# Second layer of a graph stack: attention weights a step later, updates two, half of the moments taken one layer earlier

## The chip, the cores and the metric

One core of a Trainium2 chip runs the whole kernel. The metric is device time in microseconds. TensorE does matrix products, VectorE (DVE), ScalarE (ACT) and GpSimd (POOL) the rest; each takes its own instructions in order and waits on semaphores for the others.

## The reference

64 graphs of 128 nodes with 256 features pass through four layers; each adds to x what it makes of h = relu(layernorm(x)). The second layer is the one at issue:

```python
h  = einsum(h, W); s1 = h @ a1; s2 = h @ a2
e  = leaky_relu(s1[:, :, None] + s2[:, None, :], 0.2) * mask
att = softmax(e, axis=2)
x  = x + elu(att @ h + beta * h)
```

The first layer is (adjT * q k^T) / row norm @ v, the third a normalised adjacency times h times a weight plus a bias, the fourth masked attention with 8 heads. All are float32 to the outside.

## The kernel before, in words

All of x lies in SBUF (`xs`). The graphs are worked in 32 pairs, p = 0 to 31, one layer after the other. There is no scheduler: the order on each engine is the order in which the step functions write their calls, and semaphores that count pairs tie the engines together. Several pairs are in flight, since an engine's step p handles p on one item and p - 1, p - 3 on others.

**Layer norm ahead.** For each pair VectorE takes `moments` (L114, two bn_stats), `mean_variance` (L120) and `root_argument` (L127, two small operations on mean and variance); GpSimd takes the inverse root by a power of -0.5 (`inverse_root` L140) and centres and scales (`centre` L223, two instructions of 128x256) into one of two buffers `xnb`; TensorE transposes, ScalarE takes the relu.

**First layer** (from L276). VectorE's step (L628): low part of the relu (L578), low part of the turned relation (L590), moments three pairs ahead, mask (L583), update of x (L600), low part of the values (`low_v` L595). TensorE's (L375) is t_product, turn, turn_relation, values (which needs `low_v` of the pair before), relation, outputs. VectorE's steps from p = 7 run in a hardware loop (L647), as do TensorE's and ScalarE's. GpSimd's step (L508) has the root, the norm's root, the centring. The last three steps of VectorE (L650 on) take the second layer's moments of pairs 0, 1 and 2.

**Second layer** (from L668), all written out. Per step p:
- TensorE (L714): `product(p)`, transposes of the attention weights of p - 2 (`turn_prob`), transposes of pair p + 1 (`turn`), `spread(p)` (transposes that lay out s2; it waits for ScalarE's copy of the product and for VectorE's masked scores of p - 1), `attend(p - 2)`.
- ScalarE (L772): copy of the product (`copy_h` L742, which writes `val`), copy of the turned weights, relu of the next pair, `elu_negative(p - 3)`, `softmax_exp(p - 1)`, `elu_exp(p - 3)`.
- VectorE (L859): `mask_max(p - 1)` (masked scores L832, leaky L837 whose two inputs are both `masked_e`, maximum L840), moments, aggregate and arguments of pair p + 3, reciprocal (L844), attention weights (L850, two instructions, inputs `exp_e` and `beta_ident`), update `elu(p - 4)` (L856, one input in PSUM).
- GpSimd (L812): root of pair p + 2, centring of it, `add(p - 4)` (L810: x plus exponential, 128x512, both in SBUF).

`leaky_e`, `exp_e` and `att` are single buffers. The central lines are:

```python
if p >= 1:
    mask_max(p - 1)
dve.wait_ge(freed, when)
moments(dve, ahead, step_sem, (p + 1) % 2)
mean_variance(dve, ahead, step_sem, (p + 1) % 2)
root_argument(dve, ahead, step_sem, ready_sem, (p + 1) % 2)
if p >= 1:
    inverse(p - 1)
    attention(p - 1)
if p >= 4:
    elu(p - 4)
```

## Time and profile before

| what | value |
|---|---|
| runs | 752.18 us median of 3 (751.97 to 753.36) |
| the profiled execution | 750.46 us |
| its span | 748.7 us |
| busy, share of the span | TensorE 94%, VectorE 84%, ScalarE 76%, GpSimd 63% |
| first layer | to about 179 us |
| second layer | about 179 to 323 us |

A profile is one execution. Its rows give when an instruction (or a run of like ones, xN) started and how long it took; neighbours on one engine can overlap a little, so the distance from start to start is what an instruction costs its engine. In brackets stands how long the engine had been idle before, and who released it.

### The profile page before, as it was taken

Reading aid. Unit: us, or ns where it says so; the run is one execution under the profiler, and the core shown is the slowest. Engines: PE = TensorE matmul, PEld = TensorE weight load, DVE = VectorE, ACT = ScalarE, POOL = GpSimd, SP = SyncE. Lnnn points to the kernel's source line nnn. Section 1 sums busy time; section 2 is a strip of 40 time slices with the busy share of each in tenths; the row PEclk is TensorE's granted clock in tenths of the full one; section 3 lists DMA queues with packets and bytes.
Section 4 is the critical chain, followed back from the end, with each engine's and each line's share of the span. In section 5 each row is a group of like instructions: output and inputs, shape, how many; then the busy total and the mean of one; then the engine's idle time right before and its main releaser. Section 6 shows DMA issues by size and latency. Waiting matters only on the chain.

```text
span 748.7 us, 22968 instructions
## 1 busy us (share of the span) xinstructions
PE 705.6 (94%) x6938; PEld 653.9 (87%) x6938; DVE 626.1 (84%) x2648; ACT 566.9 (76%) x1900; POOL 473.3 (63%) x610
## 2 busy tenths in 40 slices
PE   6999999998999999779998999999999999999995
PEld 5999999997777777679998899999999999999984
DVE  5888778776899999879998888888888888888863
ACT  3665655654777787747664999999999999999985
POOL 2445445445578778478884766667666676667652
PEclk9999999999999999989999999999999999999999
DMA  7222300000000000000000000000000000000001
GB/s 235 94 84 92 98 0 0 0 0 1 1 1 2 1 2 1 0 1 0 0 0 1 17 16 29 28 28 22 20 28 28 28 15 28 28 28 28 14 29 44
DMA packets 21683, 20.16 MB, mean 27 GB/s; under 512 B 2432, under 2 KB 21632, under 8 KB 21632
## 3 DMA queue, kind: packets, MB, share of 16 engines
q1 hardware_dynamic: 19440, 18.16, 7.6%
q10 hardware_dynamic: 2192, 1.44, 0.7%
q8 instruction: 17, 0.28, 0.2%
q14 instruction: 34, 0.28, 0.1%
HBM read 11.21 MB, written 8.39 MB: 26 GB/s over the span
## 4 chain that ended last, share of the span: by engine, by line
PE 76%; DVE 16%; issue 3%; ACT 2%; POOL 1%; DMA 1%; DVEq 0%; POOLq 0%; ACTq 0%
PE bank L255 42%; PE bank L1076 8%; PE bank L1068 5%; PE bank L1086 4%; PE bank L325 4%; PE bank L154 4%; PE bank L235 3%; PE bank L335 3%; DVE stats L117 3%; DVE xs L856 2%; DVE masked_e L832 2%; DVE leaky_e L837 2%; DVE att L850 2%; DVE small L840 2%; PE bank L245 1%
## 5 line engine op out<-in xcount | busy, mean ns | idle before, releaser
L1146 ACT ACTIVATE prob<-wide,small 128x128 f32<-128x128 f32 x512 | 199.1, 395 | 19.8 <-DVE small L1233 19.8
L1198 POOL TENSOR_TENSOR prob<-prob,small 128x512 f32<-128x512 f32 x128 | 133.3, 1042 | 108.1 <-DVE small L1247 108.1
L143 POOL TENSOR_TENSOR rstd<-vare,mhalf 128x2 f32<-128x2 f32 x128 | 88.8, 694 | 60.0 <-DVE vare L132 60.0
L1233 DVE CUSTOM_DVE_ANT_0 wide<-bank,mbias 128x128 f32<-128x128 f32 x512 | 116.1, 283 | 10.0 <-PE bank L1068 10.0
L226 POOL TENSOR_SCALAR xn<-xs,nmean,rstd 128x256 f32<-128x256 f32 x184 | 101.3, 561 | 11.2 <-POOL rstd L143 10.6
L117 DVE BATCH_NORM_STATS2 stats<-xs 128x6 f32<-128x256 f32 (+1 forms) x256 | 95.5, 415 | 5.7 <-DMA xs<-in_x_dram 4.5
L1146 ACT ACTIVATION_READ_ACCUMULATOR prob<-wide,small 128x1 f32 x512 | 98.3, 192 | 0.0
L1153 ACT COPY probT<-bank 128x512 f32<-128x512 f32 x128 | 72.0, 588 | 6.2 <-PE bank L1076 1.3
L1076 PE MATMUL bank<-ident,prob 128*128 128x128 f32 x512 | 73.9, 276 | 2.3 <-POOL prob L1198 2.3
L492 POOL TENSOR_TENSOR rnorm<-norm,mhalf 128x2 f32<-128x2 f32 x32 | 22.1, 690 | 79.3 <-ACT relsq L433 79.3
L1076 PEld LDWEIGHTS bank<-ident,prob 128*128 128x128 f32 x512 | 57.0, 140 | 9.6 <-issue 5.9
L245 PE MATMUL bank<-w,hT 128*128 128x258 f32 x256 | 61.3, 381 | 1.2 <-DVE xs L604 1.0
L255 PE MATMUL bank<-w,yTs 128*128 128x256 f32 x384 | 55.9, 297 | 4.5 <-DVE xs L980 4.5
L154 PE MATMUL bank<-ident,xn 128*128 128x128 f32 x376 | 56.8, 274 | 0.0
L245 PEld LDWEIGHTS bank<-w,hT 128*128 128x128 f32 x256 | 48.3, 190 | 8.9 <-DVE xs L604 1.2
L255 PE MATMUL bank<-wo,oTs 128*128 128x256 f32 x384 | 53.8, 289 | 2.2 <-DVE oTs L1256 2.2
L255 PEld LDWEIGHTS bank<-w,yTs 128*128 128x128 f32 x384 | 50.1, 199 | 6.0 <-DVE yTs L975 4.8
L255 PE MATMUL bank<-hTs,wq 128*128 128x256 f32 x384 | 53.2, 287 | 0.2 <-DVE hTs L1251 0.2
L255 PE MATMUL bank<-wv,hTs 128*128 128x256 f32 x384 | 52.9, 286 | 0.0
L255 PEld LDWEIGHTS bank<-wo,oTs 128*128 128x128 f32 x384 | 47.2, 188 | 6.3 <-DVE oTs L1256 2.7
L255 PE MATMUL bank<-hTs,wk 128*128 128x256 f32 x384 | 50.7, 281 | 0.0
L422 ACT CAST oTs<-bank 128x512 fp32r<-128x512 f32 x32 | 18.8, 589 | 40.6 <-PE bank L335 40.6
(141 smaller groups left out, 1823.6 us busy)
## 6 DMA issues: line engine op xcount, KB each, us to landing
out_dram<-xs SPq DMA_DIRECT2D x32, 256.0 KB, 2.1
xs<-in_x_dram SPq DMA_DIRECT2D x29, 256.0 KB, 2.7
xs<-in_x_dram ACTq DMA_DIRECT2D x1, 512.0 KB, 7.4
xs<-in_x_dram ACTq DMA_DIRECT2D x1, 256.0 KB, 3.7
wq<-in_L_gnn_Wq_dram SPq DMA_DIRECT2D x1, 256.0 KB, 3.3
wk<-in_L_gnn_Wk_dram ACTq DMA_DIRECT2D x1, 256.0 KB, 4.6
wv<-in_L_gnn_Wv_dram SPq DMA_DIRECT2D x1, 256.0 KB, 5.9
w<-in_L_gnn_W_dram SPq DMA_DIRECT2D x1, 256.0 KB, 7.2
```

Of the source, the lines that this page charges most:

```text
L117: ins = nc.vector.bn_stats(stats[:, b, g, :], x_of(p, g))
L143: nc.gpsimd.tensor_tensor(rstd[:, b, :], vare[:, b, :], mhalf[:, :], ALU.pow).then_inc(rstd_ready, 1)
L154: ins = nc.tensor.transpose(pe_ps[:, c * 2 * N + g * N:c * 2 * N + (g + 1) * N], src[:, g, c * 128:(c + 1) * 128], ident[:, :])
L226: ins = nc.gpsimd.tensor_scalar(xnb[b][:, g, :], x_of(p, g), nmean[:, b, g:g + 1], rstd[:, b, g:g + 1], ALU.add, ALU.mult)
L245: ins = nc.tensor.matmul(ps_g, hT[:, c, g, :], weight[:, c, :], start=(c == 0), stop=(c == C - 1))
L255: ins = nc.tensor.matmul(ps, lhsT(a, c), rhs(b, c), start=(n == 0), stop=(n == len(terms) - 1))
L1068: ins = nc.tensor.matmul(SS[r][:, (g * C + c) * N:(g * C + c + 1) * N], qT[rows_r, c, g, :], kT[rows_r, c, g, :], start=True, stop=True)
L1076: ins = nc.tensor.transpose(PT[r % 2][:, i * N:(i + 1) * N], prob[:, r, i, :], ident[:, :])
L1146: ins = nc.scalar.activation(prob[:, r, i, :], wide[:, r, i, :], ACT.Exp, bias=nmax[r][:, i:i + 1], scale=-1.0, accum_out=rsum[r][:, i:i + 1])
L1153: nc.scalar.copy(probT[:, r, :, :].rearrange("p i n -> p (i n)"), PT[r % 2][:, :]).then_inc(pt_ready, 1)
L1198: nc.gpsimd.tensor_tensor(prob[:, r, :, :], prob[:, r, :, :], rinv[r].unsqueeze(2).to_broadcast([128, QUAD, N]), ALU.mult).then_inc(prob_r ...
L1233: nc.vector.tensor_tensor_reduce(out=wide[:, r, i, :], in0=SS[r][:, i * N:(i + 1) * N], in1=mbias[:, :], scale=-1.0, scalar=3e38, op0=ALU. ...
```

## The change

The second layer's steps reach further back: TensorE turns and attends p - 3 instead of p - 2, ScalarE's ELU parts are those of p - 4, VectorE's update is that of p - 6, GpSimd's add that of p - 5. `leaky_e`, `exp_e`, `att`, the maxima and the sums get two buffers each. VectorE's step becomes: update, masked scores of p - 1, reciprocal of p - 2, leaky of p - 1, attention weights of p - 2, maximum of p - 1, and then moments: of the odd pairs alone, one graph per step, with aggregate and arguments in even steps. The moments of the even pairs are taken by VectorE in the first layer, behind each odd step (x of that pair is final by then), and GpSimd takes their roots four pairs at a time, in the first layer too. GpSimd's step in the second layer is: root (odd p only), add, centring. VectorE's hardware loop in the first layer is written out.

```diff
+        mhalf = sb("mhalf", [128, 8])
+        stats_even = sb("stats_even", [128, 2, 6])
+        mv_even = sb("mv_even", [128, PAIRS // 2, 2, 2])
+        vare_even = sb("vare_even", [128, PAIRS])
+        nmean_even = sb("nmean_even", [128, PAIRS])
+        rstd_even = sb("rstd_even", [128, PAIRS])
...
-        leaky_e = sb("leaky_e", [128, 2, N])
+        leaky_b = [sb(f"leaky_e{b}", [128, 2, N]) for b in range(2)]
...
-        exp_e = sb("exp_e", [128, 2, N])
-        att = sb("att", [128, 2, N])
+        exp_b = [sb(f"exp_e{b}", [128, 2, N]) for b in range(2)]
+        att_b = [sb(f"att{b}", [128, 2, N]) for b in range(2)]
...
+        def root_even(pool, q):
+
+            pool.wait_ge(l1_even_stats, q + 1)
+            part = slice(8 * q, 8 * q + 8)
+            nc.gpsimd.tensor_tensor(rstd_even[:, part], vare_even[:, part], mhalf[:, :], ALU.pow).then_inc(l1_even_root, 1)
+
+        def root_odd(pool, p):
+
+            inverse_root(pool, p // 2, l1_stats_ready, l1_rstd_ready, (p // 2) % 2)
+
+        def centre_first(pool, p, turned, freed):
+
+            if p % 2:
+                b = (p // 2) % 2
+                pool.wait_ge(l1_rstd_ready, p // 2 + 1)
+                scalars = [(nmean[:, b, g:g + 1], rstd[:, b, g:g + 1]) for g in range(2)]
+            else:
+                pool.wait_ge(l1_even_root, p // 8 + 1)
+                scalars = [(nmean_even[:, p + g:p + g + 1], rstd_even[:, p + g:p + g + 1]) for g in range(2)]
+            pool.wait_ge(turned, freed)
+            for g in range(2):
+                ins = nc.gpsimd.tensor_scalar(xnb[p % 2][:, g, :], x_of(p, g), *scalars[g], ALU.add, ALU.mult)
+            ins.then_inc(l1_xn_ready, 1)
+
+        def moments_even(dve, k):
+
+            dve.wait_ge(l0_x_done, 2 * k + 1)
+            if k > 0:
+                dve.wait_ge(l1_even_step, 2 * k)
+            for g in range(2):
+                ins = nc.vector.bn_stats(stats_even[:, g, :], x_of(2 * k, g))
+            ins.then_inc(l1_even_step, 1)
+            dve.wait_ge(l1_even_step, 2 * k + 1)
+            for g in range(2):
+                ins = nc.vector.bn_aggr(mv_even[:, k, g, :], stats_even[:, g, :])
+            ins.then_inc(l1_even_step, 1)
+            if k % 4 == 3:
+                q, pairs = k // 4, slice(k - 3, k + 1)
+                dve.wait_ge(l1_even_step, 2 * k + 2)
+                mean, var = (mv_even[:, pairs, :, i].rearrange("p k g -> p (k g)") for i in range(2))
+                part = slice(8 * q, 8 * q + 8)
+                nc.vector.scalar_tensor_tensor(nmean_even[:, part], mean, -2.0, mean, ALU.mult, ALU.add)
+                nc.vector.scalar_tensor_tensor(vare_even[:, part], var, EPS, var, ALU.add, ALU.max).then_inc(l1_even_stats, 1)
+
+        def moments_odd(dve, i, g):
+
+            b = i % 2
+            if g == 0 and i < 2:
+                dve.wait_ge(l0_xn_ready, PAIRS - 1 + i)
+            elif g == 0:
+                dve.wait_ge(l1_xn_ready, 2 * i - 2)
+            ins = nc.vector.bn_stats(stats[:, b, g, :], x_of(2 * i + 1, g))
+            if g == 1:
+                ins.then_inc(l1_step, 1)
+                dve.wait_ge(l1_step, 2 * i + 1)
+                for g in range(2):
+                    ins = nc.vector.bn_aggr(mv[:, b, g, :], stats[:, b, g, :])
+                ins.then_inc(l1_step, 1)
+                root_argument(dve, i, l1_step, l1_stats_ready, b)
 
         def gather_nodes(pe, ps, p, src, xn_ready):
...
                 for p in range(1, PAIRS - 2):
                     step(p, p % 2)
+                    if p % 8 == 1 and p > 1:
+                        root_even(pool, p // 8 - 1)
                 for n in range(2):
-                    inverse_root(pool, n, l1_stats_ready, l1_rstd_ready, n)
                     inverse_norm(PAIRS - 3 + n)
-                    pool.wait_ge(tr_done, PAIRS - 1 + n)
-                    centre(pool, n, n, l1_rstd_ready, l1_xn_ready)
+                    if n % 2:
+                        root_odd(pool, n)
+                    centre_first(pool, n, tr_done, PAIRS - 1 + n)
                 inverse_norm(PAIRS - 1)
+                root_even(pool, PAIRS // 8 - 1)
...
-                with dve.Fori(3, PAIRS // 2 - 2) as j:
-                    step(2 * j + 1, 1)
-                    step(2 * j + 2, 0)
+                    if p % 2:
+                        moments_even(dve, p // 2)
+                for p in range(7, PAIRS - 3):
+                    step(p, p % 2)
+                    if p % 2:
+                        moments_even(dve, p // 2)
...
                     low_v(p)
-                    if n < 2:
-                        dve.wait_ge(xn_ready, p + 2)
-                        layer_norm_stats(dve, n, l1_step, l1_stats_ready, n)
+                    if n != 1:
+                        moments_even(dve, p // 2)
+                    else:
+                        moments_odd(dve, 0, 0)
+                        moments_odd(dve, 0, 1)
                 relation_low(PAIRS - 1)
-                dve.wait_ge(l1_xn_ready, 1)
-                layer_norm_stats(dve, 2, l1_step, l1_stats_ready)
+                moments_odd(dve, 1, 0)
                 update(PAIRS - 1)
...
                 def step(p):
                     product(p)
-                    if p >= 2:
-                        turn_prob(p - 2)
+                    if p >= 3:
+                        turn_prob(p - 3)
                     if p + 1 < PAIRS:
                         turn(p + 1)
                     else:
                         gather_nodes(pe, HT, 0, xn, l2_xn_ready).then_inc(l2_yt_done, 1)
                     spread(p)
-                    if p >= 2:
-                        attend(p - 2)
+                    if p >= 3:
+                        attend(p - 3)
...
-                turn_prob(PAIRS - 2)
-                attend(PAIRS - 2)
+                for p in (PAIRS - 3, PAIRS - 2):
+                    turn_prob(p)
+                    attend(p)
                 turn_prob(PAIRS - 1)
...
                     act.wait_ge(nmax_ready, p + 1)
-                    act.wait_ge(prob_ready, since(p))
-                    for g in range(2):
-                        ins = nc.scalar.activation(exp_e[:, g, :], leaky_e[:, g, :], ACT.Exp, bias=nmax[:, g:g + 1],
-                                                   accum_out=rsum[:, g:g + 1])
+                    act.wait_ge(prob_ready, since(p - 1))
+                    for g in range(2):
+                        ins = nc.scalar.activation(exp_b[p % 2][:, g, :], leaky_b[p % 2][:, g, :], ACT.Exp,
+                                                   bias=nmax_b[p % 2][:, g:g + 1], accum_out=rsum_b[p % 2][:, g:g + 1])
                     ins.then_inc(exp_ready, 1)
...
                 def step(p):
                     copy_h(p)
-                    if p >= 2:
-                        copy_pT(p - 2)
+                    if p >= 3:
+                        copy_pT(p - 3)
                     if p + 1 < PAIRS:
...
-                    if p >= 3:
-                        elu_negative(p - 3)
+                    if p >= 4:
+                        elu_negative(p - 4)
                     if p >= 1:
                         softmax_exp(p - 1)
-                    if p >= 3:
-                        elu_exp(p - 3)
+                    if p >= 4:
+                        elu_exp(p - 4)
...
-                copy_pT(PAIRS - 2)
+                copy_pT(PAIRS - 3)
                 softmax_exp(PAIRS - 1)
                 act.wait_ge(l2_yt_done, 1)
                 nc.scalar.copy(yT_high[0], HT[:, :]).then_inc(l2_high_ready, 1)
+                elu_negative(PAIRS - 4)
+                elu_exp(PAIRS - 4)
+                copy_pT(PAIRS - 2)
                 elu_negative(PAIRS - 3)
                 elu_exp(PAIRS - 3)
...
                 for p in range(PAIRS + 1):
+                    if p + 2 >= PAIRS:
+                        root_and_shift(pool, p + 2 - PAIRS, l2_stats_ready, l2_rstd_ready, l2_shift_ready, p % 2)
+                    elif p % 2:
+                        root_odd(pool, p + 2)
+                    if p >= 5:
+                        add(p - 5)
                     if p + 2 < PAIRS:
-                        inverse_root(pool, p + 2, stats_ready, rstd_ready, p % 2)
-                        pool.wait_ge(tr_done, p + 1)
-                        centre(pool, p + 2, p % 2, l1_rstd_ready, l1_xn_ready)
-                    else:
-                        root_and_shift(pool, p + 2 - PAIRS, l2_stats_ready, l2_rstd_ready, l2_shift_ready, p % 2)
-                    if p >= 4:
-                        add(p - 4)
+                        centre_first(pool, p + 2, tr_done, p + 1)
+                add(PAIRS - 4)
                 add(PAIRS - 3)
                 root_and_shift(pool, 3, l2_stats_ready, l2_rstd_ready, l2_shift_ready, 1)
                 add(PAIRS - 2)
...
-                def mask_max(p):
...
+
+                def leaky(p):
                     dve.wait_ge(e_ready, p + 1)
-                    dve.wait_ge(exp_ready, since(p))
-                    nc.vector.scalar_tensor_tensor(leaky_e[:, :, :], masked_e[:, :, :], ALPHA, masked_e[:, :, :], ALU.mult,
+                    dve.wait_ge(exp_ready, since(p - 1))
+                    nc.vector.scalar_tensor_tensor(leaky_b[p % 2][:, :, :], masked_e[:, :, :], ALPHA, masked_e[:, :, :], ALU.mult,
                                                    ALU.max).then_inc(leaky_ready, 1)
+
+                def maximum(p):
                     dve.wait_ge(leaky_ready, p + 1)
-                    nc.vector.tensor_reduce(nmax, leaky_e[:, :, :], AX_X, ALU.max, negate=True).then_inc(nmax_ready, 1)
+                    nc.vector.tensor_reduce(nmax_b[p % 2], leaky_b[p % 2][:, :, :], AX_X, ALU.max, negate=True).then_inc(nmax_ready, 1)
 
                 def inverse(p):
                     dve.wait_ge(exp_ready, p + 1)
-                    nc.vector.reciprocal(rinv, rsum).then_inc(rinv_ready, 1)
+                    nc.vector.reciprocal(rinv, rsum_b[p % 2]).then_inc(rinv_ready, 1)
...
-                    dve.wait_ge(pt_done, since(p))
...
+                    dve.wait_ge(pt_done, since(p - 1))
+                    for g in range(2):
+                        ins = nc.vector.scalar_tensor_tensor(att_b[p % 2][:, g, :], exp_b[p % 2][:, g, :], rinv[:, g:g + 1],
+                                                             beta_ident[:, :], ALU.mult, ALU.add)
                     ins.then_inc(prob_ready, 1)
+
+                def scores(p):
+                    masked(p)
+                    if p >= 1:
+                        inverse(p - 1)
+                    leaky(p)
+                    if p >= 1:
+                        attention(p - 1)
+                    maximum(p)
 
...
                 def step(p):
-                    ahead, step_sem, ready_sem, freed, when = p + 3, dstep, stats_ready, xn_ready, p + 2
-                    if p + 3 >= PAIRS:
-                        ahead, step_sem, ready_sem = p + 3 - PAIRS, l2_step, l2_stats_ready
-                        if ahead == 2:
-                            freed, when = l2_xn_ready, 1
+                    if p >= 6:
+                        elu(p - 6)
                     if p >= 1:
-                        mask_max(p - 1)
-                    dve.wait_ge(freed, when)
-                    moments(dve, ahead, step_sem, (p + 1) % 2)
-                    mean_variance(dve, ahead, step_sem, (p + 1) % 2)
-                    root_argument(dve, ahead, step_sem, ready_sem, (p + 1) % 2)
-                    if p >= 1:
-                        inverse(p - 1)
-                        attention(p - 1)
-                    if p >= 4:
-                        elu(p - 4)
+                        scores(p - 1)
+                    if p + 3 < PAIRS:
+                        if p % 2 == 0:
+                            moments_odd(dve, p // 2 + 1, 1)
+                        elif p + 4 < PAIRS:
+                            moments_odd(dve, p // 2 + 2, 0)
+                    else:
+                        ahead = p + 3 - PAIRS
+                        if ahead < 2:
+                            dve.wait_ge(l1_xn_ready, PAIRS - 2 + 2 * ahead)
+                        else:
+                            dve.wait_ge(l2_xn_ready, 1)
+                        layer_norm_stats(dve, ahead, l2_step, l2_stats_ready, ahead % 2)
 
                 for p in range(PAIRS):
                     step(p)
-                mask_max(PAIRS - 1)
+                elu(PAIRS - 6)
+                scores(PAIRS - 1)
+                elu(PAIRS - 5)
                 inverse(PAIRS - 1)
```

Left out are the declarations of semaphores, the two roots that now name two columns of `mhalf`, and places where only a buffer's name changes.

## Rows read from the trace of the kernel before

**Rows 1.** Busy times, 5 to 178 us; at the end clock, DMA share, GB/s

```profile
5.00:178.00 173.00, 170.07 (x1434) 168.23 (x1435) 137.52 (x419) 103.05 (x297) 79.69 (x131) 1.00 0.20 60
```

**Rows 2.** Chain of waits, 200 to 300 us, shares by line

```profile
by line: DVE stats L117 16.1%; DVE xs L856 15.1%; DVE masked_e L832 13.2%; DVE leaky_e L837 10.8%; DVE small L840 10.1%; issue 10.0%; DVE att L850 9.6%; DVE mv L124 6.2%; DVE vare L132 3.5%; DVE small L844 2.1%; DVE nmean L131 1.2%; PE bank
```

**Rows 3.** Timeline, second layer: start us, us, engine, line, operation

```profile
282.63 0.44 DVE L837 SCALAR_TENSOR_TENSOR leaky_e<-masked_e 128x256 f32<-128x256 f32 x1
...
283.10 0.42 DVE L840 TENSOR_REDUCE small<-leaky_e 128x2 f32<-128x256 f32 x1
283.44 0.74 DVE L117 BATCH_NORM_STATS2 stats<-xs 128x6 f32<-128x256 f32 x2
...
284.29 0.25 DVE L124 BATCH_NORM_AGGREGATE mv<-stats 128x2 f32<-128x6 f32 x2
...
284.72 0.16 DVE L844 RECIPROCAL small<-small 128x2 f32<-128x2 f32 x1
284.88 0.69 POOL L143 TENSOR_TENSOR rstd<-vare,mhalf 128x2 f32<-128x2 f32 x1 [0.68 <-DVE vare L132]
284.91 0.61 DVE L850 SCALAR_TENSOR_TENSOR att<-exp_e,small,beta_ident 128x128 f32<-128x128 f32 x2
285.44 0.68 DVE L856 SCALAR_TENSOR_TENSOR xs<-bank,xs 128x512 f32<-128x512 f32 x1
...
285.75 1.09 POOL L226 TENSOR_SCALAR xn<-xs,nmean,rstd 128x256 f32<-128x256 f32 x2 [0.18 <-POOL rstd L143]
...
286.05 0.60 DVE L832 SCALAR_TENSOR_TENSOR masked_e<-bank,val,adj_sb 128x128 f32<-128x128 f32 x2
...
286.68 0.44 DVE L837 SCALAR_TENSOR_TENSOR leaky_e<-masked_e 128x256 f32<-128x256 f32 x1
...
286.81 1.44 POOL L810 TENSOR_TENSOR xs<-xs,exp_u 128x512 f32<-128x512 f32 x1
```

**Rows 4.** Timeline, second layer: copies of the product, first to last (32)

```profile
181.81 0.59 ACT L742 COPY val<-bank 128x516 f32<-128x516 f32 x1 [4.08 <-PE bank L245]
...
188.19 0.59 ACT L742 COPY val<-bank 128x516 f32<-128x516 f32 x1 [1.34 <-PE bank L245]
...
192.02 0.59 ACT L742 COPY val<-bank 128x516 f32<-128x516 f32 x1 [1.71 <-PE bank L245]
...
192.66 0.19 PEld L710 LDWEIGHTS bank<-ident,val 128*128 128x128 f32 x2 [0.26 <-ACT val L742]
...
306.03 0.59 ACT L742 COPY val<-bank 128x516 f32<-128x516 f32 x1
```

**Rows 5.** Timeline, 194 to 197 us, VectorE beside GpSimd

```profile
194.86 0.84 DVE L850 SCALAR_TENSOR_TENSOR att<-exp_e,small,beta_ident 128x128 f32<-128x128 f32 x2
194.87 1.26 POOL L226 TENSOR_SCALAR xn<-xs,nmean,rstd 128x256 f32<-128x256 f32 x2 [0.18 <-POOL rstd L143]
...
196.10 1.27 POOL L810 TENSOR_TENSOR xs<-xs,exp_u 128x512 f32<-128x512 f32 x1
196.25 1.39 DVE L837 SCALAR_TENSOR_TENSOR leaky_e<-masked_e 128x256 f32<-128x256 f32 x1
```

**Rows 6.** Timeline, end of the second layer

```profile
312.30 0.42 DVE L840 TENSOR_REDUCE small<-leaky_e 128x2 f32<-128x256 f32 x1
...
313.54 0.56 ACT L794 CAST yTs<-bank 128x512 fp32r<-128x512 f32 x1
...
320.27 0.63 ACT L770 ACTIVATE exp_u<-neg_u 128x512 f32<-128x512 f32 x1
...
320.98 1.29 POOL L810 TENSOR_TENSOR xs<-xs,exp_u 128x512 f32<-128x512 f32 x1 [0.75 <-ACT exp_u L770]
```

**Rows 7.** Timeline, one first-layer step

```profile
96.28 1.67 PE L255 MATMUL bank<-wv0T,hTs 128*128 128x256 f32 x12
...
97.03 0.69 DVE L580 SCALAR_TENSOR_TENSOR yTs<-bank,yTs 128x512 fp32r<-128x512 f32 x1 [0.85 <-ACT yTs L408]
```

**Rows 8.** Timeline, first product of the second layer

```profile
179.76 2.01 PE L245 MATMUL bank<-w,hT 128*128 128x258 f32 x8 [1.05 <-DVE xs L604]
```

15 lines of the change are left out of this document (7 added, 8 removed).

## The prediction

> **What bounds the kernel now.** I read the busy times by stretch first. From 5 to 178 us, the first layer, TensorE works 170 of 173 us, VectorE 138 and GpSimd 80 [rows 1]: VectorE may be given work there until it makes TensorE late. From 200 to 300 us, the second layer, the chain of waits names VectorE's instructions one after another [rows 2], so this stretch is what the change works on. Then the timeline of one second-layer step gives the price of each item by the distance from start to start [rows 3]: leaky 0.47, maximum 0.34, moments 0.85, aggregate and the two small root arguments 0.43, reciprocal 0.19, attention weights 0.53, ELU update 0.61, masked scores 0.63, together 4.05 us with no gap. GpSimd's root sits idle 0.68 us for VectorE's arguments in it [rows 3]: GpSimd starts at a fixed place of VectorE's order. Last, the steps before the updates begin show what is under VectorE: from copy to copy of the product 192.02 - 188.19 = 3.83 us pass, and the weight load of the spread waits at 192.66 for ScalarE's copy [rows 4]. TensorE's own order (product, copy, spread, attend, next product) holds that loop, and the change does not shorten it.
>
> **The change, part by part.** Sums are made against the profiled execution, 750.46 us (span 748.7 and 1.76 around it); the median of the runs shown is 1.72 above it, which I add at the end.
>
> *Second layer, VectorE's work.* Half of the moments leave it. What stays per step: update 0.61, masked scores to leaky 0.63 (the reciprocal now lies inside this wait), leaky to attention about 0.35 (0.43 long, less the 0.08 by which neighbours that don't depend on each other overlap, as the maximum's 0.42 takes 0.34), attention 0.53, maximum 0.34: 2.46. Even steps add one half of the moments and its wait, 0.85 - 0.34 = 0.51, and 0.43 for the rest, 0.94; odd steps 0.34 [rows 3]. The mean is 3.10 us instead of 4.05. Unhindered, the bound becomes the 3.83 of [rows 4], and no less.
>
> *The layer's length unhindered.* From the first copy of the product to the 32nd it is 306.03 - 181.81 = 124.2 us; the first two distances are (188.19 - 181.81) / 2 = 3.19 [rows 4]. After: three early steps (attend starts a step later), 3 x 3.19 + 28 x 3.83 = 116.8. That is -7.4.
>
> *GpSimd's new order.* Now its add (128x512, two SBUF inputs) waits only for ScalarE's exponential, and centring follows it directly. What VectorE issues meanwhile decides. The trace holds the collision: the add started at 196.10 and took 1.27; leaky, issued 0.15 later with both inputs in SBUF, took 1.39 instead of 0.43 and ended 0.27 after the add's end [rows 5]. The two attention instructions at 194.86 and the two centrings at 194.87 alternated: 0.84 instead of 0.61, 1.26 instead of 1.09 [rows 3, 5]. Where leaky is issued first, the add pays 0.17: at 286.81 it lasts 1.44, leaky having begun 0.13 before [rows 3]. The Trainium skill says the same (SBUF — State Buffer, on the shared port pair): a VectorE instruction with two SBUF inputs and a GpSimd instruction that reads SBUF exclude each other for a whole instruction, and the second fully blocks. By a milder reading, both sharing and each losing 0.17, the step would stay at 3.83; these rows side with the block.
>
> I now place the two engines, with M the start of a maximum. ScalarE's next work after the exponentials starts 1.24 after it (313.54 - 312.30), and an add starts 0.71 after the start of its exponential (320.98 - 320.27) [rows 6]: add at M + 1.95. VectorE reaches leaky at 0.34 + 0.34 + 0.61 + 0.63 = M + 1.92 after an odd step's half of moments, and at 0.34 + 0.94 + 0.61 + 0.63 = M + 2.52 after an even one's.
> - Even: the root for the next odd pair starts 0.16 behind the arguments (284.88 against 284.72), M + 1.44, lasts 0.69 [rows 3], and pushes the add to 2.13, so that it ends at 3.40. Leaky is blocked from 2.52 on. Behind the add's end come leaky 0.27, centring, attention, centring, attention in turns (2 x 0.55 and 2 x 0.14, half of leaky's 0.27 for half of its columns), less 0.10 per centring whose start-up runs while it waits, and the next maximum starts 0.08 before the last one ends: 1.37. Next M at 4.77.
> - Odd: leaky wins by 0.03, ends at about 2.35; the add ends at 1.95 + 1.44 = 3.39, holding back attention; then attention 0.14, centring 0.45, attention 0.14, less 0.08: next M at 4.04 to 4.1. If the add wins: 1.95 + 1.27 + 1.37 = 4.59.
>
> Mean (4.77 + 4.1) / 2 = 4.43 us. VectorE would need M no more than 3.83 apart to stay unhindered, and from either place it gets further behind, so the collisions hold each other up. The layer: 3 x 3.19 + 3 x 3.83 + 25 x 4.43 = 131.8, which is +7.6. With the add winning on odd steps too, 4.68 and +13.9.
>
> *First layer, moments of even pairs.* Behind each odd step stand 0.85 + 0.28 of moments and aggregate; VectorE is idle 0.85 per step before the low part at 97.03, so low_v ends at 96.18 and could have handed over 0.08 sooner, at 96.10 [rows 7]. From there 0.85 and two aggregates of about 0.18 (0.25, less 0.08 of overlap) bring the low part to 97.13: 0.1 late. Every fourth time the arguments make it 0.35. All that follows on VectorE up to the next low_v moves with it, and TensorE's values start at 96.28, 0.10 after low_v's end [rows 7], some 0.05 of it slack: 12 x 0.04 and 3 x 0.30, +1.4 us. Bounds: 0, if the slack is more, and 16 x 0.35 = 5.6. The roots of four pairs at once (128x8) aren't in the trace; one takes between the 0.69 of a pair's root [rows 3] and four of those, 2.8. Four of them lie in the 93 us in which GpSimd idles there [rows 1], right behind a centring: I take nothing; without that cover the next centring would be late, at worst by 2.8 us three times.
>
> *The seam.* Pair 30's moments now stand before relation_low(31): 0.85 + 0.28 + 0.16 = 1.29 us later than now. Outputs, update and the first product at 179.76, which waited for VectorE's update, follow [rows 8]: +1.3. The two sets of moments behind it that are gone held nobody up.
>
> *The tail.* ScalarE gets three more instructions there, none longer than the 0.63 of an exponential [rows 6], against one cheaper last step for VectorE: 0, between -0.5 and +1.9. Double buffers cost no instruction, and VectorE's first-layer loop written out is taken at nothing, as the written-out second layer runs without a gap [rows 3].
>
> Sum: 7.6 + 1.4 + 1.3 + 0 = +10.3, so 760.8 for the profiled execution and **762.5 us** for the median.
>
> **The rivals.**
> A (the forecast): VectorE is held up by GpSimd in every second step at least. For it: [rows 5] and the nearly equal clocks 1.92 and 1.95. Against it: it rests on differences of 0.03 to 0.5 us in places the trace has not shown together.
> B, faster: TensorE and the copy set the step at 3.83. It needs the blocks to cost VectorE less than 3.83 - 3.10 = 0.73 us a step; that holds if leaky and attention fall into GpSimd's gap, 3.83 - 1.27 - 1.09 = 1.47 us long. They need 0.35 + 0.53 = 0.9, but attention can't start before the exponentials are through, half a microsecond before the add. -7.4 + 1.4 + 1.3 = -4.7: 747.5 us.
> C, between: even steps collide and odd ones run at the 3.83, or both engines settle with one block of 0.96 (1.39 - 0.43) a step; 3.10 + 0.96 = 4.06. Then 21.1 + 25 x 4.06 = 122.6, -1.6, and with the seam and the first layer +1.1: 753.3 us.
> D: more of the first layer is lost than I say, up to 4 us on top of any of these.
>
> **How the numbers follow.** A 0.56, B 0.27, C 0.17; D widens each. A spans 757 (4.3 us a step, no loss in the first layer) to 770 (4.68 and D in part). A measurement of this kernel tells about 0.2%, 1.5 us, from no change. C gives half of its chance to slower, 0.06 to same and the rest to faster; B gives 0.02 to same. Faster 0.28, same 0.09, slower 0.63. The range reaches from below B, 746, to 770.
>
> **What would show it.** In the second layer of the changed kernel, A: leaky instructions over 1 us, attention pairs over 0.8, adds at 1.27, copies of the product 4.4 us apart in a pattern of two, the chain on VectorE and GpSimd. B: leaky at 0.43 throughout, 3.83 apart, the chain on TensorE and the copy. In the first layer: idle before the low part gone on every second step, and steps as long as now but for four that are 0.3 us longer. At the seam, the second layer's first product 1.3 us later against the layer's last steps. If leaky is long and the steps are 3.83 all the same, VectorE's slack was larger than I count, and the forecast is wrong there; if GpSimd waits for something else than the exponential, my placing of the add is.

## The result, and the profile after

The changed kernel takes 757.12 us (median of 12 runs, 754.6 to 758.33) against 752.08 for the kernel before on the same chip (12 runs, 750.73 to 754.15): a ratio of 1.0059 [1.0047, 1.0071], slower by 0.6%. The forecast had slower as its likeliest outcome at 762.5, and its range held the time, but its largest term has the wrong sign.

The page of the kernel after: busy times and chain. The two windows are the stretches of [rows 1] and [rows 2]; the columns are busy time of TensorE, weight loads, VectorE, ScalarE, GpSimd, then clock.

```profile
span 755.9 us, 22749 instructions
PE 713.8 (94%) x6938; PEld 662.5 (88%) x6938; DVE 639.9 (85%) x2624; ACT 565.6 (75%) x1900; POOL 472.8 (63%) x598
PE 80%; DVE 12%; issue 5%; ACT 2%; DMA 1%; POOL 0%; ACTq 0%; DVEq 0%; POOLq 0%
```

```profile
5.00:178.00 173.00, 170.45 (x1432) 168.12 (x1432) 148.65 (x477) 102.48 (x294) 83.72 (x132) 1.00 0.20 61
200.00:300.00 100.00, 95.60 (x512) 78.64 (x511) 97.64 (x274) 80.98 (x229) 74.34 (x87) 1.00 0.00 1
```

Against [rows 1] VectorE has 148.65 us of work in the first layer where it had 137.52, and TensorE is as busy as before. In the second layer VectorE is busy 97.64 of 100 us, although it was given a quarter less to do: a blocked instruction counts as busy. The chain of the same stretch, which answers to [rows 2], names the attention weights first:

```profile
by line: DVE att L932 22.3%; issue 20.6%; PE bank L311 10.5%; DVE masked_e L910 9.5%; DVE stats L287 6.5%; DVE xs L947 6.3%; DVE small L922 6.3%; PE bank L756 5.8%; PE bank L159 2.6%; PE bank L783 2.6%; DVE mv L292 2.6%; PE bank L772 1.5%; 
```

Where the time went is read from distances between starts of the same instructions in both profiled executions (span 748.7 and 755.9; us). The last column is the fastest version tried, experiment e3 below. Copy stands for ScalarE's copy of the product; the third layer is counted from the last update of the second to the fourth layer's first queries (`qT`), and the fourth from its first to its last.

| stretch | before | after | e3 |
|---|---|---|---|
| start to first mask of the first layer | 16.91 | 17.51 | 16.98 |
| first layer, first mask to last | 158.10 | 158.68 | 158.67 |
| seam, last mask to first copy of the product | 6.79 | 10.40 | 6.78 |
| second layer, first copy to last | 124.22 | 120.44 | 116.88 |
| tail, last copy to last update | 16.28 | 19.53 | 15.46 |
| third layer | 79.82 | 80.24 | 80.17 |
| fourth layer | 320.94 | 321.33 | 321.74 |
| from there to the end | 25.61 | 27.74 | 26.52 |

The second layer did become shorter, by 3.8 us; the seam took 3.6 of it back and the tail 3.3. Timeline of one pair of second-layer steps in the kernel after (start us, us, engine, line, operation), to be laid beside [rows 3, 5]:

```profile
264.55 0.41 DVE L922 TENSOR_REDUCE small<-leaky_e 128x2 f32<-128x256 f32 x1
...
265.92 0.70 POOL L148 TENSOR_TENSOR rstd<-vare,mhalf 128x2 f32<-128x2 f32 x1 [0.50 <-DVE vare L137]
...
266.59 1.26 POOL L887 TENSOR_TENSOR xs<-xs,exp_u 128x512 f32<-128x512 f32 x1
...
266.99 1.15 DVE L917 SCALAR_TENSOR_TENSOR leaky_e<-masked_e 128x256 f32<-128x256 f32 x1
...
267.84 1.39 POOL L257 TENSOR_SCALAR xn<-xs,nmean,rstd 128x256 f32<-128x256 f32 x2
...
268.06 0.75 DVE L932 SCALAR_TENSOR_TENSOR att<-exp_e,small,beta_ident 128x128 f32<-128x128 f32 x2
...
268.73 0.41 DVE L922 TENSOR_REDUCE small<-leaky_e 128x2 f32<-128x256 f32 x1
...
270.61 0.42 DVE L917 SCALAR_TENSOR_TENSOR leaky_e<-masked_e 128x256 f32<-128x256 f32 x1
270.66 1.50 POOL L887 TENSOR_TENSOR xs<-xs,exp_u 128x512 f32<-128x512 f32 x1 [1.42 <-ACT exp_u L844]
270.95 1.63 DVE L932 SCALAR_TENSOR_TENSOR att<-exp_e,small,beta_ident 128x128 f32<-128x128 f32 x2
...
272.50 0.41 DVE L922 TENSOR_REDUCE small<-leaky_e 128x2 f32<-128x256 f32 x1
```

Both collisions of the forecast are there, in the forecast order. In the even step (maximum at M = 264.55) the root comes at M + 1.37 (forecast 1.44), pushes the add to M + 2.04 (2.13), and leaky, issued at M + 2.44 (2.52), lasts 1.15 and ends 0.29 behind the add. In the odd step leaky gets in 0.05 us before the add and lasts 0.42, and the attention weights pay: 1.63 for the two. But the steps are 268.73 - 264.55 = 4.18 and 272.50 - 268.73 = 3.77 us, where 4.77 and 4.1 were forecast.

The copies of the product don't show this pattern at once. Three are 3.19 us apart, the next eight steps are 3.83, one is 3.88, eighteen alternate between 3.80 and 4.17 (mean 3.98), and the last is 4.70. Meanwhile VectorE falls behind: its maximum starts 4.62 us after the copy of the same pair at the 5th pair, 5.35 at the 7th, and 6.2 from the 13th to the 29th. So VectorE is slower than 3.83 from the first blocks on, and TensorE goes on at 3.83 until the distance between them is used up.

Timelines of the seam in the kernel after, VectorE and then TensorE; the last row answers to [rows 8]:

```profile
178.37 0.74 DVE L266 BATCH_NORM_STATS2 stats_even<-xs 128x6 f32<-128x256 f32 x2
...
179.59 0.42 DVE L661 TENSOR_TENSOR rels<-bank,rels 128x256 fp32r<-128x256 f32 x1
```

```profile
180.15 1.62 PE L401 MATMUL bank<-oTs,rels 128*128 128x256 f32 x6 [2.60 <-DVE rels L661]
182.82 1.66 PE L311 MATMUL bank<-w,hT 128*128 128x258 f32 x3 [1.05 <-DVE xs L673]
```

Busy times by stretch of the kernel after, at the seam and in the tail (clock is the third number from the right):

```profile
180.00:186.00 6.00, 4.80 (x14) 3.89 (x15) 2.03 (x9) 0.00 (x0) 3.16 (x4) 0.50 0.00 0
316.00:323.00 7.00, 5.09 (x19) 4.62 (x20) 4.41 (x13) 5.90 (x12) 3.43 (x4) 0.51 0.00 1
```

The moments of pair 30 take 179.59 - 178.37 = 1.22 us ahead of the relation's low part, as forecast. TensorE then waits 2.60 us instead of 1.40, and from there to 186 us its granted clock is 0.50, the lower level (1.2 GHz); before, the same stretch had 1.00. The six products of the outputs take 1.62 instead of 0.95, and the first copy of the product comes 3.6 later against the last mask, not 1.3. In the tail the last three leaky instructions are blocked. Timeline of the kernel after, copy of the last product and the two engines behind it, beside [rows 4, 6]:

```profile
307.03 0.56 ACT L816 COPY val<-bank 128x516 f32<-128x516 f32 x1
...
312.67 1.26 POOL L887 TENSOR_TENSOR xs<-xs,exp_u 128x512 f32<-128x512 f32 x1
...
312.81 1.40 DVE L917 SCALAR_TENSOR_TENSOR leaky_e<-masked_e 128x256 f32<-128x256 f32 x1
...
314.66 0.41 DVE L922 TENSOR_REDUCE small<-leaky_e 128x2 f32<-128x256 f32 x1
...
317.91 2.08 PE L756 MATMUL bank<-val,attT 128*128 128x256 f32 x4 [2.69 <-ACT attT L821]
```

From the last copy to the last maximum it is 7.63 us where it was 312.30 - 306.03 = 6.27 [rows 4, 6]: +1.36. From there to the last update it is 11.90 us where it was 10.00: +1.9. One attend takes 2.08 at the clock of 0.51, where the layer's others take 1.03 to 1.13.

### The profile page after: what moved, and what is told of

Same layout as the page of the kernel before. It is cut to its first block, busy times and chain, and to the rows that moved or that the text cites. A ratio compares the mean times of both kernels' runs of the same rounds, so it can differ in the third digit from the quotient of the medians.

```text
span 755.9 us, 22749 instructions
## 1 busy us (share of the span) xinstructions
PE 713.8 (94%) x6938; PEld 662.5 (88%) x6938; DVE 639.9 (85%) x2624; ACT 565.6 (75%) x1900; POOL 472.8 (63%) x598
## 3 DMA queue, kind: packets, MB, share of 16 engines
q10 hardware_dynamic: 2192, 1.44, 0.6%
## 4 chain that ended last, share of the span: by engine, by line
PE 80%; DVE 12%; issue 5%; ACT 2%; DMA 1%; POOL 0%; ACTq 0%; DVEq 0%; POOLq 0%
PE bank L321 42%; PE bank L1169 8%; PE bank L1161 5%; PE bank L1179 4%; PE bank L159 4%; PE bank L391 4%; DVE att L932 3%; PE bank L301 3%; PE bank L401 3%; PE bank L311 3%; DVE masked_e L910 1%; PE bank L756 1%; DVE small L922 1%; DVE xs L947 1%; PE bank L372 1%
## 5 line engine op out<-in xcount | busy, mean ns | idle before, releaser
L148 POOL TENSOR_TENSOR rstd<-vare,mhalf 128x2 f32<-128x2 f32 x112 | 78.2, 698 | 42.8 <-DVE vare L137 42.6
L122 DVE BATCH_NORM_STATS2 stats<-xs 128x6 f32<-128x256 f32 (+1 forms) x192 | 71.6, 415 | 6.1 <-DMA xs<-in_x_dram 5.0
L232 POOL TENSOR_SCALAR xn<-xs,nmean,rstd 128x256 f32<-128x256 f32 x120 | 65.4, 555 | 5.5 <-POOL rstd L148 5.5
L311 PE MATMUL bank<-w,hT 128*128 128x258 f32 x256 | 63.1, 389 | 1.3 <-DVE xs L673 1.1
L887 POOL TENSOR_TENSOR xs<-xs,exp_u 128x512 f32<-128x512 f32 x32 | 43.4, 1356 | 24.5 <-ACT exp_u L844 24.5
L321 PE MATMUL bank<-wo,oTs 128*128 128x256 f32 x384 | 56.0, 297 | 2.2 <-DVE oTs L1349 2.2
L321 PEld LDWEIGHTS bank<-wo,oTs 128*128 128x128 f32 x384 | 49.1, 195 | 6.3 <-DVE oTs L1349 2.7
```

What stands on the lines that cost most here:

```text
L122: ins = nc.vector.bn_stats(stats[:, b, g, :], x_of(p, g))
L148: nc.gpsimd.tensor_tensor(rstd[:, b, :], vare[:, b, :], mhalf[:, 0:2], ALU.pow).then_inc(rstd_ready, 1)
L232: ins = nc.gpsimd.tensor_scalar(xnb[b][:, g, :], x_of(p, g), nmean[:, b, g:g + 1], rstd[:, b, g:g + 1], ALU.add, ALU.mult)
L311: ins = nc.tensor.matmul(ps_g, hT[:, c, g, :], weight[:, c, :], start=(c == 0), stop=(c == C - 1))
L321: ins = nc.tensor.matmul(ps, lhsT(a, c), rhs(b, c), start=(n == 0), stop=(n == len(terms) - 1))
L887: nc.gpsimd.tensor_tensor(x_pair(p), x_pair(p), exp_u[p % 2][:, :, :], ALU.add).then_inc(added, 1)
```

## The experiments

All diffs are against the changed kernel. The first four ask what sets the step of 3.98 us (the mean of 4.18 and 3.77) and what the seam is worth; the later ones separate the parts of the change.

**e1, the seam alone.** Pair 30's moments go behind the last update.

```diff
-                    if n != 1:
+                    if n == 0:
                         moments_even(dve, p // 2)
-                    else:
+                    elif n == 1:
                         moments_odd(dve, 0, 0)
                         moments_odd(dve, 0, 1)
...
                 update(PAIRS - 1)
+                moments_even(dve, PAIRS // 2 - 1)
```

> Pair 30's moments are moved behind the last update of the first layer, so relation_low(31) stands behind low_v(31) again. Theory S (the seam is late because TensorE waits 2.60 us for relation_low there, and its clock falls to 1.2 GHz behind that idle time): the idle time before the last outputs returns to about 1.4 us, the clock stays at 2.4 GHz, outputs take 0.95 instead of 1.62 and the first product 2.0 instead of 3.74; from the last mask to the first copy of the product 10.4 becomes about 6.9 us, and the kernel gains about 3.5 us, 753.6. Rival (only the 1.2 us of moments count, the clock falls there by itself): 10.4 becomes 9.2 and the kernel gains 1.2, 756.

Measured: 754.05 us (12 runs), ratio 1.0037 [1.0022, 1.0053]. Timeline of e1's TensorE at the seam:

```profile
178.39 0.95 PE L401 MATMUL bank<-oTs,rels 128*128 128x256 f32 x6 [1.40 <-DVE rels L661]
180.37 2.01 PE L311 MATMUL bank<-w,hT 128*128 128x258 f32 x8 [1.04 <-DVE xs L673]
```

The seam is back at 6.78 us, at full clock, and the layer stays at 120.43. The profiles differ by 4.6 us in span, the ratios by 0.22%, 1.7 us: the changed kernel's profile lies above its median (757.7 and 757.12) and e1's below (753.11 and 754.05), which makes 1.5 of the difference. So the seam is worth about 2 us of the 5 lost, less than the 3.5 expected, and the intervals of e1 and of the changed kernel overlap.

**e2, the add held.** In step p GpSimd's add now also waits for the attention weights of pair p - 2, which VectorE writes in the same step, so it can start only when VectorE has left leaky and attention.

```diff
                     if p >= 5:
+                        pool.wait_ge(prob_ready, p - 1)
                         add(p - 5)
```

> GpSimd's add in the second layer also waits for VectorE's attention weights of the same step, so it can't run beside leaky and attention. Theory L (collisions of the add and the centrings with VectorE's instructions that read two SBUF inputs hold VectorE back; 4.17 and 3.80 us in turn): leaky 0.43 and attention halves 0.35 throughout, copies of the product 3.83 apart in every step, the layer's 31 distances 117 instead of 120.4 us; the blocked leaky of 1.4 in the last three steps goes too, 1 us of the tail; in all -4 to -5 us, 752.5. Rival T (TensorE or ScalarE sets the step anyway and the blocks lie in slack): distances stay 3.98 on average. Rival H (holding the add makes the update and then attend late): steps over 4.0.

Measured: 747.07 us (10 runs), ratio 0.9940 [0.9922, 0.9957]: faster than before. VectorE's timeline, then GpSimd's:

```profile
262.42 0.43 DVE L918 SCALAR_TENSOR_TENSOR leaky_e<-masked_e 128x256 f32<-128x256 f32 x1
262.76 0.61 DVE L933 SCALAR_TENSOR_TENSOR att<-exp_e,small,beta_ident 128x128 f32<-128x128 f32 x2
263.28 0.41 DVE L923 TENSOR_REDUCE small<-leaky_e 128x2 f32<-128x256 f32 x1
...
264.75 0.69 DVE L948 SCALAR_TENSOR_TENSOR xs<-bank,xs 128x512 f32<-128x512 f32 x1 [0.72 <-POOL xs L887]
...
266.24 0.42 DVE L918 SCALAR_TENSOR_TENSOR leaky_e<-masked_e 128x256 f32<-128x256 f32 x1
...
267.11 0.41 DVE L923 TENSOR_REDUCE small<-leaky_e 128x2 f32<-128x256 f32 x1
```

```profile
263.45 1.27 POOL L887 TENSOR_TENSOR xs<-xs,exp_u 128x512 f32<-128x512 f32 x1 [0.82 <-DVE att L933]
264.70 1.09 POOL L257 TENSOR_SCALAR xn<-xs,nmean,rstd 128x256 f32<-128x256 f32 x2
```

In the steady steps nothing is blocked any more: leaky 0.42, attention 0.61, add 1.27, centring 1.09, and the step is 267.11 - 263.28 = 3.83, in all but the first three, which are 3.19 long, and the last. The maximum stays 3.59 us behind its copy. The layer is 116.91 us, against 116.8 in the forecast's unhindered sum; the tail goes from 19.53 to 15.45. The update now waits 0.72 for the add, and that costs nothing, since VectorE has time over. The kernel is 5 us faster than was expected of it: 1 us had been expected of the tail. From the end of attention at 263.37 to the next leaky at 266.24 there are 2.87 us, and GpSimd's 1.27 + 1.09 = 2.36 fit in.

**e3, both.**

> Both edits. If the two are independent, the gains add: 757 - 3.5 - 4.5 = about 749 us, less than the kernel before (752). If the seam only moved the clock's fall elsewhere, or the tail eats the layer's gain, it ends at 752 or above.

Measured: 744.08 us (6 runs, 743.15 to 745.23), ratio 0.9894 [0.9871, 0.9916]. It is faster than both kernels, and 5 us faster than expected. Its chain from 200 to 300 us:

```profile
by line: PE bank L311 45.3%; PE bank L757 25.2%; PE bank L784 11.2%; PE bank L159 11.2%; PE bank L773 5.7%; issue 0.7%; DVE att L934 0.6%; DVE small L924 0.3%
```

That is TensorE's own loop, as the forecast's rival B had it. Taking the late seam away brings 0.46% here, and since e3's interval ends just below the start of e2's, that gain is shown. Whether it is larger than the 0.22% of e1 these intervals don't tell.

**e4, a small add.** Holding the add also delays the update and shifts GpSimd. To see that the add itself is the obstacle, it is cut to 2 columns per graph and not held. This leaves most of the exponential of ELU out of x.

```diff
-                    nc.gpsimd.tensor_tensor(x_pair(p), x_pair(p), exp_u[p % 2][:, :, :], ALU.add).then_inc(added, 1)
+                    nc.gpsimd.tensor_tensor(xs[:, 2 * p:2 * p + 2, 0:2], xs[:, 2 * p:2 * p + 2, 0:2],
+                                            exp_u[p % 2][:, :, 0:2], ALU.add).then_inc(added, 1)
```

> The changed kernel with GpSimd's add in the second layer cut from 256 to 2 columns of each graph (the exponential part of the ELU is left out of the rest of x). Theory L: with no long add, only centrings can block, at most 0.55 at a time: leaky 0.43 to 0.7, steps of 3.83, copies from the first to the last 117 us. Rival T: steps stay at 4.17 and 3.80.

Measured: 744.27 us, one run; layer 117.44, tail 14.35, leaky 0.42 and attention 0.60 but for one attention early in the layer. VectorE's and TensorE's work is that of the changed kernel, so the 3.0 us of the layer and 5.2 of the tail come with the add's length. The 0.53 us by which the layer is longer than e2's all lie in its first step, 3.75 against 3.19, into which the low clock of the seam reaches; behind it every step is as long as e2's to 0.01. So the centrings, which still run freely, cost the layer nothing once the add is out of the way.

**e5, centring ahead of the add.**

```diff
-                    if p >= 5:
-                        add(p - 5)
                     if p + 2 < PAIRS:
                         centre_first(pool, p + 2, tr_done, p + 1)
+                    if p >= 5:
+                        add(p - 5)
```

> The changed kernel with GpSimd's step as root, centring, add instead of root, add, centring, nothing held. Theory L: behind an even step the add starts near M + 3.2, behind leaky and attention; VectorE meets centrings alone there: leaky below 1 us, steps 3.83 to 3.9, first to last copy 117 to 118.5; the kernel 749 to 750 with the late seam. Rival (the order of add and centring does not matter, GpSimd is as busy either way): 120.4 us and 757.

Measured: 754.4 us (9 runs), ratio 1.0040 [1.0025, 1.0054], where 749 to 750 had been expected: a miss. The copies are 3.83 apart from the 4th to the 18th step, then 3.86 and 3.97 in turn, layer 118.30; the tail is 18.98. VectorE's timeline late in the layer:

```profile
280.36 0.56 DVE L917 SCALAR_TENSOR_TENSOR leaky_e<-masked_e 128x256 f32<-128x256 f32 x1
...
283.99 1.31 DVE L917 SCALAR_TENSOR_TENSOR leaky_e<-masked_e 128x256 f32<-128x256 f32 x1
```

The order alone moves the collision without removing it: from the 10th on, every second leaky still meets the add. VectorE's own steps alternate between 3.59 and 4.25 from then on, mean 3.92, while the copies are still 3.83 apart; the maximum slips from 4.62 us behind its copy (5th pair) to about 6 (20th). So the copies at 3.83 don't show an unhindered VectorE, only that its delay hasn't reached TensorE yet.

**e6, the even moments twice.** In the first layer the two bn_stats of the even pairs are taken a second time, into a buffer that nobody reads, to find what more work there costs.

```diff
             for g in range(2):
                 ins = nc.vector.bn_stats(stats_even[:, g, :], x_of(2 * k, g))
+            if k < PAIRS // 2 - 2:
+                for g in range(2):
+                    ins = nc.vector.bn_stats(stats_twice[:, k, g, :], x_of(2 * k, g))
```

> The changed kernel with the even pairs' moments taken twice in the first layer (the second result is not used), 14 times 0.67 us more on VectorE. If VectorE's slack there is the 0.85 us before the low part and the first set has used it up, TensorE's values wait about 0.65 in each odd step: the first layer's masks, first to last, go from 158.7 to 167 or 168 us. If TensorE has slack of its own there, less: 160 to 163.

Measured: 762.26 us, one run; first layer 163.85, 5.2 more. VectorE's timeline:

```profile
99.12 0.74 DVE L267 BATCH_NORM_STATS2 stats_even<-xs 128x6 f32<-128x256 f32 x2
99.78 0.73 DVE L270 BATCH_NORM_STATS2 stats_twice<-xs 128x6 f32<-128x256 f32 x2
...
100.99 0.68 DVE L653 SCALAR_TENSOR_TENSOR yTs<-bank,yTs 128x512 fp32r<-128x512 f32 x1
```

Fourteen pairs at 99.78 - 99.12 = 0.66 are 9.2 us more work, and 5.2 were paid: 0.37 per pair. The first set, 15 pairs up to the last mask, costs 0.8 (158.68 against the 157.87 of e7 and e8 below, which lack it); the next one is paid for by more than half. The 163.85 lie between the two expectations, so the first set has used up most of the slack and not all of it.

**e7, all moments in the second layer, add held.** The moments and roots are put back as in the kernel before; what is left of the change is the lag and the double buffers, with e2's wait. **e8, the same without the wait.** The diff of e7 at its core (e8 lacks the wait and has the add behind the centring, as before):

```diff
-                    elif p % 2:
-                        root_odd(pool, p + 2)
+                    else:
+                        inverse_root(pool, p + 2, stats_ready, rstd_ready, p % 2)
                     if p >= 5:
+                        pool.wait_ge(prob_ready, p - 1)
                         add(p - 5)
...
-                    if p + 3 < PAIRS:
-                        if p % 2 == 0:
-                            moments_odd(dve, p // 2 + 1, 1)
-                        elif p + 4 < PAIRS:
-                            moments_odd(dve, p // 2 + 2, 0)
...
+                    dve.wait_ge(freed, when)
+                    layer_norm_stats(dve, ahead, step_sem, ready_sem, (p + 1) % 2)
```

> The weights a step later, the double buffers and the held add of e3_both, but all moments stay in the second layer, a whole pair per step, as in the kernel before. Theory L: VectorE's step is 3.10 + 0.64 = 3.74 us without blocks, still under the 3.83 of TensorE and the copy, so moving the even pairs' moments brings nothing: steps of 3.83, first to last copy 117 us; the first layer takes 158.1 as before, the seam about 6.8; the kernel about 743.5, within 1 us of e3_both. Rival M (the moved moments are what makes room): steps of 3.95 or more, 747 or above.

> As e7_all_moments_held, but GpSimd in the order of the kernel before and not held: root, centring, add. Theory L: the root waits for VectorE's arguments at M + 1.6, centring ends near M + 3.6, so leaky and attention (M + 2.86 to 3.74) run beside centrings, at most 0.1 to 0.3 a step, and the add falls behind them: steps of 3.85 to 4.0, first to last copy 117 to 121 us, no leaky over 0.7 after the first steps. The kernel 744 to 749. Rival B (without GpSimd freed of VectorE's order the step stays at 4.05): 124 us, 751.

Measured: e7 745.23 us (6 runs), ratio 0.9912 [0.9888, 0.9936], layer 117.27, every step 3.83 but the first three and the last. e8 753.89 us (12 runs), ratio 1.0031 [1.0016, 1.0047], layer 121.96, steps of 3.83 at first and 4.05 from the 11th on; 744 to 749 had been expected of it, a miss. Its layer is 2.3 us shorter than the kernel before's, but its tail is 18.96 us, 2.7 longer: as in the changed kernel, its last three leaky take 1.40 each. VectorE's timeline of e8:

```profile
263.76 0.62 DVE L909 SCALAR_TENSOR_TENSOR leaky_e<-masked_e 128x256 f32<-128x256 f32 x1
264.30 0.75 DVE L924 SCALAR_TENSOR_TENSOR att<-exp_e,small,beta_ident 128x128 f32<-128x128 f32 x2
264.97 0.41 DVE L914 TENSOR_REDUCE small<-leaky_e 128x2 f32<-128x256 f32 x1
...
269.03 0.41 DVE L914 TENSOR_REDUCE small<-leaky_e 128x2 f32<-128x256 f32 x1
```

Leaky loses 0.2 and attention 0.14 to GpSimd; 4.06 less these is about 3.72, which is below TensorE's 3.83. So with the lag alone VectorE's work, all moments included, would just fit; a third of a microsecond of blocking per step is the whole difference between 3.83 and 4.05. With the add held it does fit, and then moving half of the moments buys nothing that can be measured: e7's interval and e3's overlap. e8 also splits the 3.8 us by which the changed kernel shortened the layer: 2.3 come with the lag alone, and 1.5 with the moved moments and GpSimd's other order.

**e9 and e10, TensorE kept busy at the seam.** Two products of the identity with a 128x512 tile, into two banks that are free at that point, are put ahead of the last outputs and used by nobody; e9 is the changed kernel with them, e10 is e3 with them.

```diff
+                for k in range(2):
+                    nc.tensor.matmul(bank[6 + k][:, :], ident[:, :], w1T[:, :, :].rearrange("p c d -> p (c d)"),
+                                     start=True, stop=True)
```

> The changed kernel, late seam and all, but TensorE gets two products of 128x512 that nobody uses, ahead of the last outputs of the first layer, about 1.7 us of its 2.60 us of waiting. Nothing waits for them and the outputs can't start earlier. Theory S (at the seam the long wait costs by the clock behind it): the idle time falls to about 0.9, the clock stays at 2.4 GHz, outputs 0.95 and first product 2.0, from the last mask to the first copy of the product 10.4 becomes about 8.0, and the kernel gains about 2 us. Rival (the clock falls there whatever TensorE does in the wait): 9.4 to 10.4 as before and no gain.

> e3_both with the same two unused products. There the wait is 1.4 us and the clock did not fall in its profile; the filler covers the wait, so the seam stays at 6.8 us. If the clock falls there in a part of e3_both's runs, which one profile can't show, the median gains up to 0.5 us; otherwise 744 as e3_both.

Measured: e9 755.88 us (6 runs), ratio 1.0053 [1.0038, 1.0068]; e10 744.69 (4 runs), ratio 0.9906 [0.9891, 0.9922]. TensorE's timeline of e9:

```profile
176.90 1.88 PE L468 MATMUL bank<-w1T,ident 128*128 128x512 f32 x4
179.68 0.94 PE L401 MATMUL bank<-oTs,rels 128*128 128x256 f32 x6 [0.90 <-DVE rels L664]
181.68 2.01 PE L311 MATMUL bank<-w,hT 128*128 128x258 f32 x8 [1.05 <-DVE xs L676]
```

The filler holds the clock: outputs 0.94, product 2.01, and the seam is 8.01 us, which is the 6.79 of before and the 1.22 of moments. This splits the seam's 3.6: 1.2 is VectorE's order and 2.4 the clock (in e2, e4 and e5, where it fell only behind the outputs, the seam is 9.39, 9.81 and 9.69). In the timed runs e9 gains 0.06% on the changed kernel, within the intervals, where 2 us had been expected: the 2.4 of this profile are not shown to be lost in a typical execution. e10 brings nothing over e3, in whose profile the shorter wait of 1.40 left the clock alone.

## Why the prediction was right and wrong

**What bounds the kernel (right).** VectorE before, and TensorE with ScalarE's copy at 3.83 once VectorE is unhindered: e2, e3 and e7 run at 3.83, and the layer of e2 and e3 is 116.9, forecast 116.8.

**Collisions (mechanism right, size wrong: the step that failed).** Their places were right within 0.1 us, and e2 and e4 show that the add is their cause. The failed term is the 1.37 us that the forecast put behind the add's end in the even step: leaky 0.27, centring, attention, centring, attention, with 0.45 for each centring. Each is half of the 1.09 of [rows 3] less 0.10 for a start-up hidden in the wait, and that 0.10 stood in no row. Seen one by one (timeline of the kernel after), the first centring and the second half of attention are:

```profile
267.84 0.83 POOL L257 TENSOR_SCALAR xn<-xs,nmean,rstd 128x256 f32<-128x256 f32 x1
...
268.33 0.48 DVE L932 SCALAR_TENSOR_TENSOR att<-exp_e,small,beta_ident 128x128 f32<-128x128 f32 x1
```

The add ends at 267.85, leaky at 268.14, the first half of attention at 268.41 (0.35 long, not held), the centring at 268.67 and the second half at 268.81. So one centring comes in between, not two; it ends 0.26 behind the attention half before it and keeps the next half back by 0.13; it is the centrings that pay, 1.39 instead of 1.09. The next maximum starts 268.73 - 267.85 = 0.88 after the add's end, 0.5 sooner than forecast. In the odd step no centring comes in between, and it is 272.50 - 272.16 = 0.34 in place of 0.65 to 0.7. The mean step is 3.98 us instead of 4.43. Over the 25 steps that the forecast put at 4.43 the layer is 11.4 us shorter: 8.1 for eighteen steps at 3.98, 3.6 for the six before them that still run at 3.83 to 3.88 because VectorE's delay reaches TensorE late, and 0.3 back for a last step of 4.70. It turns +7.6 into -3.8. What ran is nearer to rival C, one block in each step, a step of 4.06 and a layer of 122.6 (measured 120.4). Of A's signs, leaky over 1 us and the pattern of two came true, 4.4 us did not.

**First layer (right).** +0.6 against the loop of before and +0.8 against e7 and e8, which are written out too and lack the moments (157.87 both); forecast 1.4, with 0 to 5.6 as bounds. By the forecast's count the slack was used up, and a second set would have cost all of its 9.2 us; e6 paid 5.2, so the slack was somewhat larger than counted.

**Seam (term too small).** The order costs 1.2, as forecast at 1.3. The clock was left out of the sum: in every profile with the longer wait (after, e2, e4, e5, e6) it fell to 0.50 behind it. In the changed kernel's profile this adds 2.4, in e2's, e4's and e5's 1.4 to 1.8; the timed difference between e1 and the changed kernel, 1.7 us, leaves room for only a part.

**Tail (wrong).** Forecast 0, between -0.5 and +1.9; the profile shows +3.3. GpSimd's adds meet leaky in the last three steps, and VectorE enters them 6.2 us behind its copies: 1.4 of the loss lies up to the last maximum. The held add brings that stretch from 7.6 to 4.3 us (e2, e3), below the 6.3 of before. The other 1.9 lie behind the last maximum. There 11.2 us are left of 11.90 with the add held, and 10.05 with the small add, against 10.00 before; so 1.1 goes with the length of the adds that are left for the end, not with ScalarE's added instructions. The rest may be the clock (0.51 from 316 to 323 us, where the profile before has 0.81): e7, whose add is held too, has it at 0.50 for 6.8 us behind its last maximum where e2 and e3 have 3.4, and takes 12.3 instead of 11.2. In e5 and e8, where the low stretch of 6.8 us begins right at the last maximum, it is 11.35. So the clock is worth up to about 1 us there, an estimate; no run changed it alone. e8 lost 2.7 in the tail with the lag alone. The forecast placed the collisions only in the steady state, and looked for the tail's cost at ScalarE.

**The sum.** By parts it was 7.6 + 1.4 + 1.3 + 0 = 10.3. The profiles show -3.8 + 0.6 + 3.6 + 3.3 = 3.7, and 3.5 more in stretches that the change does not touch: 0.6 before the first mask, 0.4 and 0.4 in the third and fourth layers, 2.1 at the end. The medians of 12 runs differ by 5.0. So "slower" came true, but of the loss forecast in the second layer's steps nothing is left; it is made of the seam, the tail, and a rest that stays open.

**What stays open.** In the last 15 us the granted clock falls twice in the profiles of the changed kernel, e1, e2, e6, e7 and e9, whose end takes 27.2 to 27.8 us, and once in e3, e5, e8 and e10 (26.4 to 26.5); the profiles of the kernel before and of e4 have no such fall ahead of the last instructions, and 25.6. Nothing of the change is there, and no run tried for the cause. Which share of executions shows the fall at the seam isn't known either, as each profile is one execution. The mean granted clock of every timed run is on record, though: 0.982 to 0.986 for the changed kernel, 0.984 to 0.989 for e1, 0.986 to 0.993 for the kernel before in e1's rounds. The three runs of each that had 0.986 took 754.6 to 755.7 us changed and 754.0 to 754.1 before. So most of the 5 us goes along with more time at the lower clock; which of it the change brings about, by its waits at the seam and in the tail, is not shown.

## What to carry to other kernels

Work taken from a bounding engine is worth only what its collisions leave. Here a lag of one step and a quarter of VectorE's work moved away gave 3.8 us together, 2.3 of them by the lag alone, and one wait that keeps GpSimd's two-input add out of VectorE's two-input instructions gave 3.5 more in the steps and 4.1 at the end; letting an engine run freely is not a gain when it shares something with the bound one. A step that looks unhindered on one engine can hide another that falls behind, so compare their distance at the start and the end of a stretch. When two engines are placed by hand, follow the pattern through the last steps too, and ask of every wait lengthened on TensorE what it does to the clock behind it.

## What the runs showed of the hardware that was not expected

- A GpSimd instruction that has started by the trace does not always hold VectorE up. The centring (two instructions) starts at 267.84, the attention weights at 268.06, and those last 0.75 together, against 0.60 unhindered; the centring stretches to 1.39 from 1.09. The Trainium skill (SBUF — State Buffer, SBUF: two separate sides) has the one that starts first keep the SBUF ports that the two engines share for its whole instruction. That holds for the add, which kept leaky until 0.29 behind its end and was itself 1.26 long. It also holds for a centring that finds VectorE free: in e8 one starts at 263.55 and lasts 0.55, and leaky, issued at 263.76, ends 0.28 behind it. The centring at 267.84 was different, since leaky, held back by the add, ran until 268.14; VectorE's next instruction, issued at 268.06, still took its usual 0.35 and the centring ended behind it. So by these rows "first" is not the start that the trace shows when a centring itself has to wait.
- An instruction with two SBUF inputs can be held for a whole add: attention's first half took 1.36 us (of the 1.63 at 270.95) when leaky had just won by 0.05.
- TensorE's granted clock fell to 0.50 (1.2 GHz) behind a wait of 2.60 us in all five profiles that have it, behind one of 1.40 in one of five (e7), and not behind 0.90, after filler products (e9). The product took 3.74 us for 2.01, the outputs 1.62 for 0.95.
- The power of -0.5 on 128x8 takes 1.64 us on GpSimd, on 128x2 0.70: eight columns cost 2.3 times two.
